# Later gate and up weight parts folded from the sum and difference of their halves; stages of the down weights moved

## The reference, cut to what matters

```
s = causal attention(xn Wq^T, xn Wk^T, xn Wv^T), 16 heads of 16, rotary positions, then Wo
h = fwht(xn * SU_ug) / 64            # Walsh-Hadamard transform over 256 features
u, g = h W_up^T * scale, h W_gate^T * scale      # 1024 each
f = fwht(silu(g) * u * SU_dp) / 64   # transform over 1024
out = x + s * silu(f W_down^T * scale)
```

## Time and profile before

| what | us |
|---|---|
| time before, median of 3 runs (lowest, highest) | 814.73 (812.35, 814.88) |
| the profiled execution's own time | 813.83 |
| its span, first to last instruction | 812.1 |
| PE busy in the span | 789.1 (97%) |
| VectorE, ScalarE, GpSimd busy | 565.2, 499.2, 411.9 |

### The profile page before, as it was taken

The page is one execution under the profiler, slowest core; times in us unless marked ns, Lnnn a source line. Parts: engine busy times, 40 slices in busy tenths (PEclk is TensorE's granted clock), DMA queues, the critical chain, the costliest instruction groups (busy, mean ns, idle before and its releaser), DMA issues. The chain is left out here.

```text
span 812.1 us, 14555 instructions
## 1 busy us (share of the span) xinstructions
PE 789.1 (97%) x5232; PEld 480.9 (59%) x5232; DVE 565.2 (70%) x1022; ACT 499.2 (61%) x686; POOL 411.9 (51%) x471
## 2 busy tenths in 40 slices
PE   9999999999989999999999999999999999999987
PEld 4678788888765455554555555555555554555534
DVE  5776545454676777777877777777777778777637
ACT  4566455463534777666777665677766667666472
POOL 2978678574642463321765434266453236736233
PEclk9999999999999999999999999999999999999999
DMA  9163444354440222333233452334344332445222
GB/s 316 70 201 105 155 156 156 105 134 151 170 119 30 65 70 62 92 102 109 93 110 108 127 170 92 94 107 130 105 123 131 105 96 94 135 123 162 84 83 72
DMA packets 61247, 95.71 MB, mean 118 GB/s; under 512 B 10552, under 2 KB 27640, under 8 KB 61176
## 3 DMA queue, kind: packets, MB, share of 16 engines
q1 hardware_dynamic: 59176, 92.42, 37.2%
q10 hardware_dynamic: 2000, 2.36, 0.8%
HBM read 57.54 MB, written 36.95 MB: 116 GB/s over the span
## 5 line engine op out<-in xcount | busy, mean ns | idle before, releaser
L1547 ACT ACTIVATE probs<-ps 128x1024 f32<-128x1024 f32 (+1 forms) x320 | 292.0, 937 | 101.7 <-PE ps L1377 99.7
L1668 DVE TENSOR_REDUCE mx<-ps 128x4 f32<-128x512 f32 (+1 forms) x192 | 215.4, 1134 | 79.3 <-PE ps L1354 49.8
L1235 POOL TENSOR_SCALAR_AFFINE_SELECT probs<-probs 128x256 f32<-128x256 f32 (+1 forms) x192 | 93.0, 487 | 261.8 <-ACT probs L1547 260.6
L1663 DVE CUSTOM_DVE_ANT_0 ps<-ps,tri 128x384 f32<-128x384 f32 (+1 forms) x256 | 154.5, 647 | 29.3 <-PE ps L1354 28.9
L1399 PE MATMUL ps<-probs,v_ones 128*32 128x512 f32 (+3 forms) x1584 | 157.0, 486 | 0.2
L1377 PE MATMUL ps<-q_s,k_s 64*128 64x512 f32 (+3 forms) x768 | 143.3, 398 | 9.2 <-DVE mx L1663 2.9
L1354 PE MATMUL ps<-k_s,q_s 48*128 48x512 f32 (+3 forms) x768 | 137.3, 382 | 4.1 <-DVE mx L1668 1.6
L1377 PEld LDWEIGHTS ps<-q_s,k_s 64*128 64x128 f32 x768 | 68.2, 184 | 105.5 <-issue 69.1
L1354 PEld LDWEIGHTS ps<-k_s,q_s 48*128 48x128 f32 x768 | 69.5, 184 | 71.4 <-ACT probs L1547 49.7
L330 PE MATMUL ps<-xh,wug_hi 128*128 128x512 f32 x256 | 105.6, 413 | 0.5 <-DVE rot L882 0.4
L385 POOL TENSOR_TENSOR a_sb<-a_sb,u_sb 128x512 f32<-128x512 f32 x64 | 82.6, 1298 | 44.7 <-ACT u_sb L358 23.3
(11 more groups left out here) (150 smaller groups left out, 1054.7 us busy)
## 6 DMA issues: line engine op xcount, KB each, us to landing
scr_qk<-kinds SPq DMA_DIRECT2D x64, 256.0 KB, 2.5
q_s<-scr_qk SPq DMA_DIRECT2D x64, 128.0 KB, 2.8
k_s<-scr_qk SPq DMA_DIRECT2D x64, 128.0 KB, 3.0
scr_heads<-o_raw SPq DMA_DIRECT2D x30, 256.0 KB, 2.1
scr_v<-v_st SPq DMA_DIRECT2D x16, 256.0 KB, 2.9
q_s<-scr_qk SPq DMA_DIRECT2D x64, 64.0 KB, 2.9
k_s<-scr_qk SPq DMA_DIRECT2D x64, 64.0 KB, 3.0
v_raw<-scr_v SPq DMA_DIRECT2D x16, 256.0 KB, 2.8
```

Source lines behind the costliest of these rows:

```text
L1235: pool.affine_select(out=part, in_=part, compare_op=ALU.is_ge, fill=0.0, base=0, pattern=pattern, channel_multiplier=-1).then_inc(cut, 1)
L1547: act.activation(probs[:, n % 2, p, :, 0:w], ps[:, bank:bank + 2, 0:w], ACT.Exp, scale=SCALE).then_inc(exp_ok, 1)
L1663: last = dve.tensor_tensor_reduce(part_of, part_of, sh.tri[:, CH - w:CH], 1.0, LOWEST, ALU.add, ALU.max, mx[:, v % 2, kind, h, i % TPC:i % ...
L1668: last = dve.tensor_reduce(out[:, :, pairs[0]:pairs[0] + n], ps[:, banks[0]:banks[0] + 2, 0:n * w].rearrange('p e (x k) -> p e x k', x=n), ...
```

## The change

W2 and W3 no longer multiply both halves twice. VectorE first writes the sum and the difference of the halves of the part (`add_halves`, two 128x512 operations each, into the space of parts 0 and 1, whose folds are done), and PE multiplies each with `had`: two fp32 matmuls where there were four. W2 moves from place 0 to place 1 of chunk 0, W4 and W5 both to place 2 of chunk 1. `fold_down(0)` moves on GpSimd from ahead of `rsqrt(1)` to place 0 of chunk 0, `fold_down(1)` to place 2 of chunk 0, and `fold_down_last` on VectorE to chunk 1, behind `turn(1, 1)` and ahead of `take_xl(2)`. The low part of Wv moves from VectorE to GpSimd, ahead of `rsqrt(1)`, and ScalarE's high part of it moves ahead of `weights_high(1)`.

```diff
-FOLDS = {(-1, 0): (0,), (-1, 1): (1,), (0, 0): (2,), (0, 2): (3,), (1, 1): (4,), (1, 2): (5,)}
+FOLDS = {(-1, 0): (0,), (-1, 1): (1,), (0, 1): (2,), (0, 2): (3,), (1, 2): (4, 5)}
...
+        sum_of = lambda i: wug[:, i - 2, 0, :]
+        difference_of = lambda i: wug[:, i, 1, :]
...  GpSimd
-            fold_down(0)
+            pool.wait_ge(wq_hi, 2)
+            pool.tensor_tensor(wqkv_lo[:, :, 2 * D:], wqkv[:, :, 2 * D:], wqkv_hi[:, :, 2 * D:].bitcast(F32),
+                               op=ALU.subtract).then_inc(wv_ok, 1)
             rsqrt(1)
-            DOWN_FOLDS = {(0, 0): (1,)}
+            DOWN_FOLDS = {(0, 0): (0,), (0, 2): (1,)}
...  PE, fold_weights
+                    if i >= 2:
+                        pe.wait_ge(added, i - 1)
                     for o in range(DC):
+                        if i >= 2:
+                            last = pe.matmul(ps[:, bank + o, :], had[:, :], difference_of(i) if o else sum_of(i), start=True,
+                                             stop=True)
+                            continue
                         pe.matmul(ps[:, bank + o, :], had[:, :], wug[:, i, 0, :], start=True, stop=False)
...  PE, ahead of values(k)
-                pe.wait_ge(wq_ok, 2)
+                pe.wait_ge(wv_ok, 1)
...  VectorE
+            def add_halves(i):
+                dve.wait_ge(ug_in[i], 32)
+                dve.wait_ge(prod, i - 1)
+                dve.tensor_tensor(sum_of(i), wug[:, i, 0, :], wug[:, i, 1, :], op=ALU.add)
+                dve.tensor_tensor(difference_of(i), wug[:, i, 0, :], wug[:, i, 1, :], op=ALU.subtract).then_inc(added, 1)
...
             for i in folds_at(-1, 1):
                 weights_low(i)
-            weights_rest(1)
             for k in range(NCHUNK):
                 if k:
                     kinds_low(k - 1, 1)
+                if k == 0:
+                    add_halves(2)
                 turn(k, 0)
                 jobs(k, 0)
+                if k == 0:
+                    add_halves(3)
                 turn(k, 1)
                 jobs(k, 1)
+                if k == 1:
+                    fold_down_last()
                 if k + 1 < NCHUNK:
                     take_xl(k + 1)
                 if k + 2 < NCHUNK:
                     variances(k + 2)
-                if k == 0:
-                    fold_down_last()
```

More of the change, by code:

```diff
@@ L449, in first_block @@
         scale_ok, had_ok, d_fold = (sem('scale_ok'), sem('had_ok'), sem('d_fold'))
-        wq_hi, wq_ok = (sem('wq_hi'), sem('wq_ok'))
-        prod, w_hi, w_lo = (sem('prod'), sem('w_hi'), sem('w_lo'))
+        wq_hi, wq_ok, wv_ok = (sem('wq_hi'), sem('wq_ok'), sem('wv_ok'))
+        prod, w_hi, w_lo, added = (sem('prod'), sem('w_hi'), sem('w_lo'), sem('added'))
+        sum_of = lambda i: wug[:, i - 2, 0, :]
+        difference_of = lambda i: wug[:, i, 1, :]
         stats_ok, moments_ok, var_ok = (sem('stats_ok'), sem('moments_ok'), sem('var_ok'))
@@ L801, in _ @@
             take_xh(0)
+            act.wait_ge(qkv_in[1], 16)
+            act.copy(wqkv_hi[:, :, 2 * D:], wqkv[:, :, 2 * D:]).then_inc(wq_hi, 1)
             for i in folds_at(-1, 1):
                 weights_high(i)
-            act.wait_ge(qkv_in[1], 16)
-            act.copy(wqkv_hi[:, :, 2 * D:], wqkv[:, :, 2 * D:]).then_inc(wq_hi, 1)
             ups = lambda k, place: [j for j in jobs_in(k, place) if j[0] == 'up']
@@ L911, in weights_low, with weights_rest @@
                 last.then_inc(w_lo, 1)
[L913 to L916, removed]
+            def weights_rest():
+                dve.wait_ge(wq_hi, 1)
+                dve.tensor_tensor(wqkv_lo[:, :, 0:2 * D], wqkv[:, :, 0:2 * D], wqkv_hi[:, :, 0:2 * D].bitcast(F32),
                                   op=ALU.subtract).then_inc(wq_ok, 1)
@@ L938, in _ @@
             dve.tensor_tensor(sh.half_both[:, :], sh.half_gate[:, :], ws_ug[:, 0:IB], op=ALU.mult).then_inc(scales_ok, 1)
-            weights_rest(0)
+            weights_rest()
             for i in folds_at(-1, 0):
```

## The result

| what | us |
|---|---|
| time after, median of 20 runs (lowest, highest) | 815.88 (814.17, 818.38) |
| time before, 20 runs beside them | 814.51 (811.45, 817.24) |
| ratio after to before, 95% interval | 1.0025 (1.0015 to 1.0036) |
| profiled execution's own time, its span | 818.38, 816.6 |

The change makes the kernel slower by 0.25%, 2.0 us by the ratio (1.2 to 2.9 by its interval; the two medians are 1.4 us apart). That is less than the 0.3% that I counted as a change, and clear of zero. The profiled execution is the slowest of its 20, so I don't read the 4.5 us between the two profiled executions as the change's.

What follows compares the result with a forecast made beforehand. PE's work plus the few waits reaching it was taken to bound the kernel; 3.4 us of work and 1.8 of waits removed against 7.3 of new waits, less rounding, gave +1.3: 815.1 to 816.0, named 815.5, range 811 to 818.

Steps and rivals of the forecast that it cites:

- rival 3: PE's clock falls in the new wait ahead of W4, slowing W4 and W5: net +2.7 us, 817.4 on the median; chance 0.25.
- Removed, 3.44 us and the waits ahead of X1 and W2: On PE, four fp32 matmuls of 0.86 us go, and waits of 1.1 (X1) and 0.3 (W2).
- VectorE takes turns with GpSimd: On SBUF-only operations each engine waits for the other's running instruction; the last down stage then ends at 47.6.
- Rival 1: Contention stretches the last down stage by nothing, or nothing anywhere: net -1.1 to -3 us, 813.4 to 811.5; chance 0.25.
- GpSimd's chain from 22.4: GpSimd works without a gap from rotate(0,0) at 22.4 through fold_down(1), ending at 42.8; X2 waits 2.4 us.
- PE's own stretch up to W4: PE's order laid out from Q0 at 15.97; Q1 starts at 29.9, four jobs end at 44.1 ahead of W4.
- W4 waits 3.5: PE waits 3.5 us ahead of W4 for the last down stage, which ends at 47.6.
- The forecast's own case, clock kept: Turns taken and clock kept: the first job behind V1 starts at 54.1, 1.3 us late; chance 0.38.
- The clock kept: PE's granted clock stays at 1.00 behind the new wait ahead of W4, so W4 and W5 run at full speed.
- The dip at 242: PE's clock fall at 242 to 246 us can vanish or lengthen, 1.7 us either way, over every case; chance 0.3.
- Rival 2: No waits arise at X2 and W4, so PE's work is saved in full: -5.2 us, 809.3; chance 0.07.

Runs made afterwards that it cites:

- e3: The changed kernel with rotate(1,0) on GpSimd waiting until the last down stage on VectorE is done; ratio to the kernel before 1.0014.
- e1: The changed kernel with 16 matmuls of zeros on TensorE ahead of its wait for the last down stage; ratio to the kernel before 1.0006.
- e6: The changed kernel with W4 and W5 moved behind V1, ahead of the jobs of place 3; ratio to the kernel before 1.0010.
- e10: The changed kernel with queries_low(0) on VectorE, W4 and W5 behind V1, and rotate(1,0) waiting for the last down stage; ratio to the kernel before 0.9981.
- e4: The changed kernel with the down weights' stages, W4 and the roots back at their old places; ratio to the kernel before 1.0016.
- e7: The changed kernel with queries_low(0) moved from GpSimd to VectorE and W4, W5 behind V1; ratio to the kernel before 0.9978.

## Why the prediction was right or wrong, point by point

The forecast was 815.5 within 811 to 818, +1.3 us, most likely within 0.3%; measured 815.88, and +2.0 us by the ratio. The ratio's interval, 1.2 to 2.9 us, holds both the forecast's +1.3 and rival 3's +2.7, so the times alone don't tell the two apart; the places do.

- *Removed, 3.44 us and the waits ahead of X1 and W2*: right. W2 takes 1.7 (21.82 to 23.54), W3 near 1.9, X1 doesn't wait.
- *VectorE takes turns with GpSimd*: right. The difference of W3's halves was done 24.8 by the sum and 25.1 by the trace; the last stage 47.6 and 47.3. Rival 1 (no turns) falls. That whole instructions alternate is read from the times (1.28, then 2.24 and 2.26); e3 shows only that the stretching comes from the GpSimd operations beside the stage. Of the Trainium skill's two readings, that of its GPSIMD Engine Reference (Specifications), where VectorE's instructions with two SBUF inputs contend as well, agrees with the 4.49 against 2.36.
- *GpSimd's chain from 22.4*: right in its length and its parts. One turn was mis-sized: I let the shift of chunk 2 wait 1.1 us for kinds_low; it ran ahead of it (34.54), so X2 waited 0.7 and not 2.4. The turn was lost one operation later, by queries_low (3.35 in place of 2.4), so that the stages behind came as forecast.
- *PE's own stretch up to W4*: the new waits add up to 7.4 and not 7.3, and 7.4 less the 5.2 gained is 2.2, not 1.3. The 0.9 called rounding is work laid out too short: W3 took 1.9 against 1.7, Q1 and K1 took 5.8 against 5.5, V0 2.95 against 2.8, the four jobs 5.8 against 5.5. It did no harm, since W4's start hangs on VectorE; with X2's shorter wait it only changed how long PE stood there.
- *W4 waits 3.5*: 3.85.
- *The forecast's own case, clock kept*: e1 is the test of it. There W4 starts at 47.33 (47.6), V1 at 51.10 (51.4) and the first job behind it at 54.00 (54.1).
- *The clock kept*: here the forecast's case failed in the profiled execution and rival 3 held in it: W4 and W5 slow, net +2.7 by its sum, +2.70 by the start of the job behind V1 (55.48 against 52.78). That it fits to the number is partly luck: W0 started 0.15 us later here, and by the distance it is +2.55. I gave it 0.25. Its price was right, its condition (a wait over 1.6 us, the idle time of the earlier trace rows) was not: the clock stayed at 1.00 behind waits of 1.73 and 1.99 us in e3 and 2.09 in e6. e1 shows that the fall is a cost of its own, 1.5 us. Whether the clock falls there in each execution isn't read directly, but the mean clocks speak for it: none of the changed kernel's 20 executions reached 1.000, the highest is 0.998, which is what one fall left in the kernel before's profiled execution; with the filler 2 of 12 reached it, in the kernel before 22 of 93.
- *The dip at 242*: gone after; in the profiled execution others came at 748 to 751 and from 809 us on. The first two weigh the same, as laid over every case; the last, worth some 1.5 us, stands in no case of mine.
- *Rival 2*: falls. It would have needed the last stage done 8 us earlier; only in e10, with GpSimd's chain shortened, V1 put ahead and the rotation held back, do saved matmuls count, and there by about 1.1 to 1.3 of the 3.4 us.

What failed is thus no step of the chain but the weight of one term, the clock: 1.5 us that I left out of the sum and kept for the range. That the median still came out at 815.88 says little for the sum, since 1.5 us is less than the spread of the runs.

## What to carry to other kernels

When the busiest engine loses work, lay out the next chain beside it, instruction by instruction, before counting the saving: here 3.4 us less of TensorE were worth nothing as long as GpSimd's chain, lengthened by the same change, set when the next fold could start. An idle gap of TensorE can be paid twice, once as a wait and once as a lower clock behind it (here 3.85 us of wait and 1.5 us of clock), so fill it. By the distance, ready work put there by a change of order (e6, 43.99) gave more than idle matmuls (e1, 45.48); by time the two aren't told apart (1.0010 and 1.0006). And where a kernel's executions scatter by 0.3%, look at the mean clock of each before calling two kernels the same: e10's lead of 3.8 us shows plainly among the executions at 1.000 and is 1.5 us in the medians. Put a two-operation job of VectorE on SBUF data where GpSimd is in a wait, or make GpSimd wait for it, if nobody stands behind.

## What the runs showed of the hardware that I had not expected

- The clock can fall behind a wait of 2.0 us (e4: 1.99, then 0.55 over 3.8 us), and can stay behind one as long (e3: 1.99, e6: 2.09, then 1.00). The length of the wait alone doesn't decide.
- A VectorE operation on 128x4 elements, with one input, took over a microsecond longer beside a GpSimd rotation (1.34 in place of 0.16, e7), so small operations are held too.
- Work that a change adds on one of two engines that take turns costs on both: the difference in add_halves(3) took 1.76 in place of 0.68, and the two operations of the rotation beside it 1.66 and 1.72 in place of 1.29.
